# A two-stage image kernel: the convolution's loop written out as 24 chunks, and half of each output store moved behind the next matrix loads

## The chip, the cores and the metric

The kernel runs on one core of a Trainium2 chip. The metric is the device time of one execution in microseconds (us), median of several runs; less is better.

## What is computed

Two layers follow each other on an input of 4 images x 48 channels x 128 x 128 in float32. The first is a windowed transformer block (layer norm, attention in 8 x 8 windows, projection, layer norm, MLP with GELU, two residuals). The second, which the change touches, is an inverted bottleneck:

```python
h = jnp.einsum('oc,bchw->bohw', w1, x)                 # 48 -> 288 channels
h = jax.nn.relu(_bn(h, g1, b1, m1, v1))
h = jax.lax.conv_general_dilated(h, wd, (1, 1), ((1, 1), (1, 1)), feature_group_count=HID, ...)   # depthwise 3x3
h = jax.nn.relu(_bn(h, gd, bd, md, vd))
h = jnp.einsum('oc,bchw->bohw', w2, h)                 # 288 -> 48 channels
return x + _bn(h, g2, b2, m2, v2)
```

## The kernel before

Three stages run one after the other: `attention` (to about 770 us of the profile), `mlp` (to about 1100 us) and `conv` (to the end). `conv` shares its block of engine programs with `mlp`.

How `conv` is tiled. Each of the 4 images is cut into two halves of 64 columns, 8 halves in all (`HALVES`), and the 288 middle channels into 3 chunks of 96 (`CHUNKS`), so there are 24 chunks. A chunk has the number k = 3 x half + c; `number(b, hx, c)` works it out from the image b, the half hx in it and the chunk c. A half is 128 patches of 8 x 8 pixels, and one matmul of the depthwise step takes one channel with a matrix of its nine taps laid out for a patch (`mats`, three tiles of 32 channels, 896 KB each to load).

What TensorE does in chunk k (`chunk`, from L1147 on): depthwise units 1 to 5 of chunk k (`depthwise`, matmuls L1134, 160 of the chunk's 192), and then, in 8 steps (`NSTEP`), it expands the patches of chunk k + 1 (L1115), turns chunk k's result (transposes L1169) and projects it (L1160). Ahead of the last projection it does depthwise unit 0 of chunk k + 1. ScalarE and VectorE empty PSUM (L882, L883, L1216), and VectorE adds each projection to the output tile `y` (called `yc` in the profile): L1253 at c = 0, L1258 at c = 1, L1256 at c = 2. At c = 0 it overwrites what the half before left, so ahead of the first and of the fifth addition (n = 0 and n = 4, `PER_BLOCK` = 4) it waits on `y_stored[0]` and `y_stored[1]`, the stores of the first and the second 64 rows.

What GpSimd (POOL) does: it scales each loaded matrix tile in place (L932, `mats_scaled`), which TensorE waits for ahead of depthwise units 0, 2 and 4 of the next chunk, and it cuts the next half's image strips (`piece`) into patches `xp` (L906), at c = 1 and c = 2.

What SyncE (SP) does is the queue that the change reorders. SP's program is one list, and a wait in it holds up all that stands behind it. In chunk k, in this order:

1. three loads of `mats` for chunk k + 1 (L1073), each when TensorE has finished the depthwise units that read the tile (2, 4 and 6 of the 6 units; `unit_ready`);
2. at c = 0 and c = 1, eight strips each of the next half (`load_pieces`, L1065), two loads a strip; the second load of the first strip waits for the landing of the third matrix tile, the others for the strip before and for the cut that frees their slot;
3. at c = 2, the output of the half: for each of two blocks of rows a wait on `y_done` and two stores of 384 KB (L1082). The second block is complete at the end of the chunk, so its stores are followed at once by the matrix loads of the next half's first chunk.

All engines take the order of chunks from one helper, `schedule` (L801). It runs image 0, 1 and 2 (six chunks each, k = 0 to 17) as a hardware loop of three rounds (`eng.Fori`, L804) with the image's number in a register, so that the waits compare with values worked out in registers, and the last image (k = 18 to 23) as written-out code with constants. TensorE's loop body is six chunks long.

Of the kernel before, what the change touches and what calls it, by code (L numbers as in the profile page):

```python
# [29 lines left out]
B, C, H, W = 4, 48, 128, 128  # L30
# [18 lines left out]
PH, PW = 8, 8  # L49
# [7 lines left out]
CHUNKS = HID1 // CH  # L57
TCH = 32
LOADS = CH // TCH
HALVES = B * 2  # L60
# [6 lines left out]
def wait(eng, sem, n):  # L67

    if not isinstance(n, int) or n >= 1:
        eng.wait_ge(sem, n)  # L70
# [680 lines left out]
def conv(nc, d):  # L751


    with ExitStack() as ctx:
# [14 lines left out]
        PART = 8  # L769
# [10 lines left out]
        y = sb("yc", [P, PR * PH, PC // 2 * PW])  # L780
# [6 lines left out]
        mats_loaded = [sem(f"mats_loaded{s}") for s in range(LOADS)]  # L787
# [6 lines left out]
        y_ready, y_done, y_stored = sem("c_y_ready"), sem("c_y_done"), [sem(f"c_y_stored{k}") for k in range(2)]  # L794
# [4 lines left out]
        NSTEP = len(STEPS)  # L799

        def schedule(eng, first, chunk):  # L801

            first()
            with eng.Fori(0, HALVES // 2 - 1, 1) as b:  # L804
                for hx in range(2):
                    for c in range(CHUNKS):
                        chunk(b, hx, c, False)
            for hx in range(2):
                for c in range(CHUNKS):
                    chunk(HALVES // 2 - 1, hx, c, hx == 1 and c == CHUNKS - 1)  # L810

        LEAD = 3
        BLOCKS = PR // PART
        PER_BLOCK = NSTEP // BLOCKS
# [7 lines left out]

        def more(b, hx):

            return not (hx == 1 and isinstance(b, int))

        FIXED = 2 + 5 + 2 + SLOTS + 1 + 2 * SLOTS

# [4 lines left out]
        def pieces_at(c):  # L833
            return range(PR // 2 * c, PR // 2 * (c + 1))

        def nth_in_slot(j):
            return slot_of[:j].count(slot_of[j])

        def place_of(j):


            s = slot_of[j]
            before = [i for i in range(j) if slot_of[i] == s]
            return s, before[-1] + 1 if before else max(i for i in range(PR) if slot_of[i] == s) + 1 - PR
# [9 lines left out]
        def number(b, hx, c):  # L854
            return 2 * CHUNKS * b + CHUNKS * hx + c
# [9 lines left out]
        def ready_before_depthwise(k):  # L865
            return ready_before_expand(k) + EXPANDS
# [31 lines left out]
        block = ctx.enter_context(nc.Block(name="mlp_conv"))  # L898
# [36 lines left out]
        def piece_rows(j):  # L935

            lo, hi = max(PH * j - 1, 0), min(PH * j + PH + 1, H)
            return lo, hi, lo - (PH * j - 1)
# [106 lines left out]
        @block.sync  # L1045
        def _(sp):
            sp.wait_ge(fixed, FIXED)
            for s in range(2):
                sp.wait_ge(img_stored[s], 32 * (STRIPS // 2))

            def load_pieces(b, hx, h, c):

                k = CHUNKS * (h - 1) + c
                for j in pieces_at(c):
                    slot, nth = place_of(j)
                    wait(sp, cut, PR * h + nth)
                    lo, hi, off = piece_rows(j)
                    for r in range(2):
                        if r and j > pieces_at(c)[0]:
                            before = slot_of[j - 1]  # L1060
                            sp.wait_ge(piece_loaded[before], 32 * (PER_HALF[before] * (h - 1) + nth_in_slot(j - 1) + 1))
                        elif r:
                            sp.wait_ge(mats_loaded[-1], 16 * (k + 1))
                        x0 = HALF * hx + HALF // 2 * r
                        sp.dma_start(piece[slot][ONE * r:ONE * r + C, off:off + hi - lo, :],  # L1065
                                     d["img_images"][:, b, lo:hi, x0:x0 + SIDE]).then_inc(piece_loaded[slot], 16)

            def chunk(b, hx, c, last):
                k = number(b, hx, c)
                if not last:  # L1070
                    for s in range(LOADS):
                        sp.wait_ge(unit_ready, ready_before_depthwise(k) + READY[DEPTHS // LOADS * (s + 1)])
                        sp.dma_start(mats[s][0:MROWS, :, :], d["taps"][LOADS * ((c + 1) % CHUNKS) + s])\  # L1073
                            .then_inc(mats_loaded[s], 16)
                if c < 2 and more(b, hx):
                    load_pieces(b + hx, 1 - hx, 2 * b + hx + 1, c)
                if c == CHUNKS - 1:
                    for block in range(BLOCKS):
                        sp.wait_ge(y_done, NSTEP * k + PER_BLOCK * (block + 1) + 1)
                        rows = slice(PH * PART * block, PH * PART * (block + 1))  # L1080
                        for r in range(2):
                            sp.dma_start(d["out"][4 * b + 2 * hx + r].rearrange("c (y x) -> c y x", y=H)[:, rows, :],  # L1082
                                         y[64 * r:64 * r + C, rows, :]).then_inc(y_stored[block], 16)

            schedule(sp, lambda: None, chunk)
            for block in range(BLOCKS):
                sp.wait_ge(y_stored[block], 32 * HALVES + 32)

        @block.tensor
        def _(pe):  # L1090
# [57 lines left out]
            def chunk(b, hx, c, last):  # L1148
# [32 lines left out]
                for n in range(NSTEP + 1):  # L1181
# [7 lines left out]
                    if n < NSTEP:  # L1189
                        turn(n)  # L1190

            schedule(pe, first, chunk)

        @block.scalar
        def _(act):
# [23 lines left out]
            def first():  # L1219
                expanded(0, range(0, EXPANDS, 2))  # L1220
                for s in range(2):
                    act.wait_ge(img_stored[s], 32 * (STRIPS // 2))

            schedule(act, first, chunk)

        @block.vector
# [111 lines left out]
```

## Time and profile before

| | |
|---|---|
| median of 3 runs | 2005.19 us (2003.86 to 2009.8) |
| the profiled execution | 2007.32 us, its span 2005.3 us |
| TensorE busy | 1913.1 us, 95% of the span |
| VectorE, ScalarE, GpSimd busy | 72%, 68%, 32% |
| granted TensorE clock, mean | 0.991 |
| DMA | 198.73 MB, 99 GB/s over the span |

The profile is of one execution, its own time beside that of its span; what is worked out from rows is worked out for it. Engines: PE is TensorE's matmuls, PEld its weight loads, PEldq, DVEq, ACTq and SPq the engines' instruction queues, where branches, register operations and DMA issues show. `<-` in a tile column reads "out from in". The chain that ended last follows the execution back from its last instruction, at each step to what released it; "issue" is time in which the engine waited for nothing that the profile shows. In the DMA view, q1 holds the transfers issued by SP, q8 and q14 ("instruction") bring the engines' own code, in packets of 16 KB and 8 KB.

### The profile page before, as it was taken

The numbers are of one execution on the slowest core, as the hardware profiler recorded it, in microseconds if no ns is written. First come the engines' busy times: TensorE is split into PE (matmuls) and PEld (weight loads), VectorE is DVE, ScalarE is ACT, GpSimd is POOL, SyncE is SP. The second block draws the span as 40 slices with busy tenths as digits, with TensorE's granted clock in tenths as the row PEclk, the third lists the DMA queues.
The fourth block names the chain that finished last, engine by engine and source line by source line (L and its number), as shares of the span: only waits on it lengthen the run. The fifth ranks groups of instructions, "written<-read, shape, count | busy, mean of one in ns | idle before, by whom it ended". The sixth has DMA issues, their size and how long they took to land.

```text
span 2005.3 us, 76491 instructions
## 1 busy us (share of the span) xinstructions
PE 1913.1 (95%) x29704; PEld 1584.4 (79%) x29704; DVE 1441.9 (72%) x2586; ACT 1365.1 (68%) x2838; POOL 647.0 (32%) x869
## 2 busy tenths in 40 slices
PE   5999999999999996999999999999999999999998
PEld 4888888888888884555555898989989898999987
DVE  4999999999999995555556556656656565566554
ACT  2888888888888884666666566656666566666655
POOL 4333333333333336023000433424334243324240
PEclk9999999999999997999999999999999999999999
DMA  2222222222222224677554345435354454455431
GB/s 65 67 76 76 76 76 75 73 77 75 76 76 76 76 71 113 159 164 156 135 134 110 95 99 132 96 100 129 92 129 98 110 132 99 92 138 101 109 95 34
DMA packets 286441, 198.73 MB, mean 99 GB/s; under 512 B 225991, under 2 KB 275672, under 8 KB 276504
## 3 DMA queue, kind: packets, MB, share of 16 engines
q1 hardware_dynamic: 282114, 189.12, 37.7%
q0 software_dynamic: 2368, 6.25, 1.8%
q8 instruction: 154, 2.52, 0.6%
q10 hardware_dynamic: 1750, 0.39, 0.1%
q14 instruction: 55, 0.45, 0.1%
HBM read 128.36 MB, written 54.72 MB: 91 GB/s over the span
## 4 chain that ended last, share of the span: by engine, by line
PE 57%; ACT 2%; issue 1%; DVE 1%; DMA 0%; SPq 0%; ACTq 0%; DVEq 0%
PE psum L1115 14%; PE psum L1134 13%; PE psum L1160 9%; PE psum L676 6%; PE psum L661 6%; PE psum L1169 5%; PE psum L650 3%; ACT h2T L1216 1%; DVE h L883 1%; DMA room<-in_ident 0%; ACT room L742 0%; DVE room L883 0%; ACT room L746 0%; ACT h L882 0%; DVE room L708 0%
## 5 line engine op out<-in xcount | busy, mean ns | idle before, releaser
L932 POOL TENSOR_TENSOR mats<-mats,dscale 112x2048 f32<-112x2048 f32 x72 | 260.8, 3622 | 350.1 <-DMA mats<-in_taps 348.1
L1115 PE MATMUL psum<-ew,xp 64*100 64x96 f32 x6144 | 322.6, 253 | 15.5 <-DVE h L883 11.1
L1216 ACT ACTIVATE h2T<-psum 96x1024 f32<-96x1024 f32 x192 | 195.8, 1020 | 189.6 <-PE psum L1169 189.6
L883 DVE TENSOR_SCALAR h<-psum 100x384 f32<-100x384 f32 x384 | 212.0, 557 | 149.8 <-PE psum L1115 139.0
L1115 PEld LDWEIGHTS psum<-ew,xp 64*100 64x100 f32 x6144 | 295.3, 165 | 25.4 <-DVE h L883 14.1
L1134 PE MATMUL psum<-h,mats 101*64 101x128 f32 x4608 | 269.4, 276 | 6.8 <-issue 5.2
L1134 PEld LDWEIGHTS psum<-h,mats 101*64 101x64 f32 x4608 | 253.9, 138 | 15.5 <-issue 6.5
L882 ACT ACTIVATE room<-psum 64x512 f32<-64x512 f32 (+1 forms) x384 | 206.3, 537 | 85.1 <-PE psum L1134 78.7
L344 PE MATMUL psum<-kb,qa 128*64 128x256 f32 x2048 | 244.6, 381 | 0.6 <-DVE prob L443 0.6
L883 DVE TENSOR_SCALAR room<-psum 64x512 f32<-64x512 f32 (+1 forms) x288 | 174.1, 604 | 72.1 <-PE psum L1134 66.1
L882 ACT ACTIVATE h<-psum 100x384 f32<-100x384 f32 x384 | 186.7, 486 | 45.8 <-PE psum L1115 33.6
L1160 PE MATMUL psum<-h2T,pw 128*64 128x128 f32 x3072 | 196.7, 277 | 19.7 <-issue 10.2
L1160 PEld LDWEIGHTS psum<-h2T,pw 128*64 128x64 f32 x3072 | 167.9, 137 | 32.1 <-ACT h2T L1216 13.7
L344 PEld LDWEIGHTS psum<-kb,qa 128*64 128x64 f32 x2048 | 140.8, 138 | 56.2 <-issue 1.9
L526 POOL TENSOR_TENSOR xn<-cen,rstd 128x192 f32<-128x192 f32 x128 | 64.7, 506 | 339.9 <-ACT rstd L499 339.9
L436 DVE TENSOR_REDUCE top<-psum 128x16 f32<-128x1024 f32 x128 | 156.7, 1224 | 6.7 <-PE psum L344 4.3
L742 ACT ACTIVATE room<-psum,room 128x512 f32<-128x512 f32 x128 | 81.2, 686 | 112.8 <-PE psum L676 112.7
L443 DVE TENSOR_TENSOR prob<-psum,top 128x1024 f32<-128x1024 f32 x128 | 155.9, 1218 | 0.1
L471 ACT ACTIVATE probT<-psum 128x512 f32<-128x512 f32 x256 | 151.3, 601 | 0.0
L396 PE MATMUL psum<-vb,probT 128*64 128x26 f32 x4096 | 143.4, 219 | 1.6 <-issue 1.0
L396 PEld LDWEIGHTS psum<-vb,probT 128*64 128x64 f32 x4096 | 129.9, 138 | 18.7 <-issue 1.2
L906 POOL COPY xp<-piece 128x400 f32<-128x400 f32 x128 | 67.6, 528 | 226.0 <-DMA piece<-img_mid 223.6
(152 smaller groups left out, 3309.8 us busy)
## 6 DMA issues: line engine op xcount, KB each, us to landing
mats<-in_taps SPq DMA_DIRECT2D x69, 896.0 KB, 6.3
tok_mid<-mid SPq DMA_DIRECT2D x128, 224.0 KB, 1.9
room<-tok_mid SPq DMA_DIRECT2D x64, 448.0 KB, 3.8
piece<-img_mid SPq DMA_DIRECT2D x196, 63.8 KB, 2.3
img_mid<-room SPq DMA_DIRECT2D x128, 97.5 KB, 2.9
kb<-kk SPq DMA_DIRECT2D x512, 24.0 KB
out<-yc SPq DMA_DIRECT2D x32, 384.0 KB, 4.3
scratch<-in_x_tokens SPq DMA_DIRECT2D x126, 96.0 KB, 2.0
```

The costliest lines, as they stand in the source:

```text
L344: mm = nc.tensor.matmul(ps_s[NT * w:NT * w + NT, p // 2, 256 * (p % 2):256 * (p % 2) + 256], qa[s][:, NT * n:NT * n + NT], kb[s][:, n, :, ...
L396: mm = nc.tensor.matmul(ps_o[NT * w:NT * w + NT, at:at + 2 * VE], probT[:, p, h, NT * w:NT * w + NT], vb[1 - s][:, p, h, w, :], start=True ...
L436: nc.vector.tensor_reduce(top[s][:, :], sc, AX_X, ALU.max).then_inc(top_done, 1)
L443: nc.vector.tensor_tensor(prob[s][:, :, :], sc, bc(top[s][:, :], 2, NT), ALU.subtract)\
L471: nc.scalar.activation(probT[:, 2 * k:2 * k + 2, :, :].rearrange("q p h n -> q (p h n)"), ps_p[:, k, :], ACT.Copy)\
L882: return nc.scalar.activation(dst, src, ACT.Relu)
L883: return nc.vector.tensor_scalar(dst, src, 0.0, None, ALU.max)
L932: nc.gpsimd.tensor_tensor(m, m, bc(scale[0:MROWS, at:at + TCH], 2, POUT), ALU.mult).then_inc(mats_scaled, 1)
L1115: mm = nc.tensor.matmul(ring[(j + u) % 4][0:PIN, p:4 * CH:4], xp[hx][rows, 2 * j + p, :], w1[rows, c, :], start=True, stop=True)
L1134: mm = nc.tensor.matmul(bank[:, n % 4:4 * PATCHES:4], mats[ch // TCH][0:PIN + 1, ch % TCH, :], h1[0:PIN + 1, ch, :], start=True, stop=True)
L1160: mm = nc.tensor.matmul(ps_y[n % 2][64 * r:64 * r + 64, at:at + PCOLS], w2[:, c, :], h2T[n % 2][:, r, at:at + PCOLS], start=True, stop=True)
L1216: nc.scalar.activation(h2T[n % 2][0:CH, :, :], turned_at(n, last)[0:CH, :, 0:POUT * PART], ACT.Copy).then_inc(copied, 1)
```

## The change

`schedule` no longer has a loop: all engines' programs for the 24 chunks are written out one after the other, with constants in place of register values. `more`, which says whether there is a next half whose strips are to be loaded, is rewritten for that, with the same meaning.

SP's stores become a function `store(h, block)`. The first block of a half is still stored at the end of SP's part of chunk c = 2. The second block is stored in the next half's first chunk: behind its three matrix loads, after a wait until the third of them has landed (`mats_loaded[-1]`), and ahead of its strip loads. The last half stores both blocks at its end as before. Nothing else is changed: the same matmuls, transfers and semaphores.

```diff
--- before.py
+++ after.py
@@ -801,13 +801,8 @@
         def schedule(eng, first, chunk):
 
             first()
-            with eng.Fori(0, HALVES // 2 - 1, 1) as b:
-                for hx in range(2):
-                    for c in range(CHUNKS):
-                        chunk(b, hx, c, False)
-            for hx in range(2):
-                for c in range(CHUNKS):
-                    chunk(HALVES // 2 - 1, hx, c, hx == 1 and c == CHUNKS - 1)
+            for k in range(HALVES * CHUNKS):
+                chunk(k // (2 * CHUNKS), k // CHUNKS % 2, k % CHUNKS, k == HALVES * CHUNKS - 1)
 
         LEAD = 3
         BLOCKS = PR // PART
@@ -822,7 +817,7 @@
 
         def more(b, hx):
 
-            return not (hx == 1 and isinstance(b, int))
+            return 2 * b + hx + 1 < HALVES
 
         FIXED = 2 + 5 + 2 + SLOTS + 1 + 2 * SLOTS
 
@@ -1065,6 +1060,15 @@
                         sp.dma_start(piece[slot][ONE * r:ONE * r + C, off:off + hi - lo, :],
                                      d["img_images"][:, b, lo:hi, x0:x0 + SIDE]).then_inc(piece_loaded[slot], 16)
 
+            def store(h, block):
+
+                k = CHUNKS * h + CHUNKS - 1
+                sp.wait_ge(y_done, NSTEP * k + PER_BLOCK * (block + 1) + 1)
+                rows = slice(PH * PART * block, PH * PART * (block + 1))
+                for r in range(2):
+                    sp.dma_start(d["out"][2 * h + r].rearrange("c (y x) -> c y x", y=H)[:, rows, :],
+                                 y[64 * r:64 * r + C, rows, :]).then_inc(y_stored[block], 16)
+
             def chunk(b, hx, c, last):
                 k = number(b, hx, c)
                 if not last:
@@ -1072,15 +1076,15 @@
                         sp.wait_ge(unit_ready, ready_before_depthwise(k) + READY[DEPTHS // LOADS * (s + 1)])
                         sp.dma_start(mats[s][0:MROWS, :, :], d["taps"][LOADS * ((c + 1) % CHUNKS) + s])\
                             .then_inc(mats_loaded[s], 16)
+                if c == 0 and k:
+                    sp.wait_ge(mats_loaded[-1], 16 * (k + 1))
+                    store(k // CHUNKS - 1, 1)
                 if c < 2 and more(b, hx):
                     load_pieces(b + hx, 1 - hx, 2 * b + hx + 1, c)
                 if c == CHUNKS - 1:
-                    for block in range(BLOCKS):
-                        sp.wait_ge(y_done, NSTEP * k + PER_BLOCK * (block + 1) + 1)
-                        rows = slice(PH * PART * block, PH * PART * (block + 1))
-                        for r in range(2):
-                            sp.dma_start(d["out"][4 * b + 2 * hx + r].rearrange("c (y x) -> c y x", y=H)[:, rows, :],
-                                         y[64 * r:64 * r + C, rows, :]).then_inc(y_stored[block], 16)
+                    store(k // CHUNKS, 0)
+                    if last:
+                        store(k // CHUNKS, 1)
 
             schedule(sp, lambda: None, chunk)
             for block in range(BLOCKS):
```

## Rows read from the trace of the kernel before

**Rows 1.** The page, parts 1 (busy, share, instructions) and 3 (queue: packets, MB, share).

```profile
PE 1913.1 (95%) x29704; PEld 1584.4 (79%) x29704; DVE 1441.9 (72%) x2586; ACT 1365.1 (68%) x2838; POOL 647.0 (32%) x869
...
q8 instruction: 154, 2.52, 0.6%
```

**Rows 2.** The chain that ended last, 1080 to 2005 us: start us, us, what.

```profile
1198.15 8.91 PE psum L1134 x160
...
1234.02 8.97 PE psum L1134 x160
...
1250.47 2.27 issue
...
1272.43 8.91 PE psum L1134 x160
...
1308.20 8.91 PE psum L1134 x160
...
1343.97 2.76 issue
...
1384.70 8.91 PE psum L1134 x160
...
1472.69 1.70 issue
...
1565.62 2.41 issue
...
1693.73 3.07 issue
...
1824.14 9.06 PE psum L1134 x160
...
1860.06 9.06 PE psum L1134 x160
...
1895.99 9.13 PE psum L1134 x160
...
1912.92 2.91 issue
...
1936.73 9.06 PE psum L1134 x160
...
1972.65 7.26 PE psum L1134 x128
```

**Rows 3.** Lines L804 and L592 (mlp's loop): durations min/median/max ns, first and last start.

```profile
L804 PEldq COMPARE_BRANCH  x3: 83/3407/3752, 1342.8 to 1786.9; - x3
...
L592 PEldq COMPARE_BRANCH  x14: 76/208/221, 823.6 to 1082.0; - x14
```

**Rows 4.** DMA, 1244 to 1249.5 us: packets and MB; every queue that moved anything.

```profile
DMA packets 171, 1.24 MB, mean 225 GB/s; under 512 B 20, under 2 KB 20, under 8 KB 20
...
q1 hardware_dynamic: 170, 1.23, 99.2%
q14 instruction: 1, 0.01, 0.7%
```

**Rows 5.** Timeline of SP's DMA issues, 1232 to 1249 us: start, us, line.

```profile
1235.34 0.83 SPq L1082 DMA_DIRECT2D out<-yc  x2
1236.30 7.07 SPq L1073 DMA_DIRECT2D mats<-in_taps  x3
```

**Rows 6.** DMA by chunk (2; then 3; then 4, two rows): KB each, median us to landing.

```profile
out<-yc SPq DMA_DIRECT2D x2, 384.0 KB, 5.3
...
mats<-in_taps SPq DMA_DIRECT2D x3, 896.0 KB, 11.8
...
q8 instruction: 5, 0.08, 1.0%
...
mats<-in_taps SPq DMA_DIRECT2D x3, 896.0 KB, 6.2
```

**Rows 7.** Timelines of VectorE and GpSimd: fifth addition of chunk 3, scalings in chunk 4.

```profile
1265.45 0.69 DVE L1253 TENSOR_TENSOR yc<-psum,xp 128x512 f32<-128x512 f32 x1 [0.44 <-PE psum L1160]
...
1284.80 7.33 POOL L932 TENSOR_TENSOR mats<-mats,dscale 112x2048 f32<-112x2048 f32 x2 [1.28 <-DMA mats<-in_taps]
```

## The prediction

> **What bounds the kernel now.** I read the page first. TensorE is busy for 1913.1 of 2005.3 us [rows 1], so only what stops TensorE, or makes its own stream longer, moves the time. The change touches the convolution alone, so I went to the chain that ended last, from 1106 us on, and used it as a ruler. A chunk k (0 to 23; k % 3 == 0 opens a half) shows there as one piece of 160 depthwise matmuls, `PE psum L1134 x160`, and the distance from one such start to the next is what a chunk costs. A chunk in which nothing goes wrong takes 1308.20 - 1272.43 = 35.77 us inside the loop, and 1860.06 - 1824.14 = 35.92 us in the six chunks that are already written out behind it [rows 2]. From chunk 2 to chunk 23 there are 21 distances, 1972.65 - 1198.15 = 774.50 us, where 21 x 35.77 = 751.17. So 23.33 us of the convolution is excess, and the change can be worth no more than that.
>
> Where the excess sits is told by the pieces called "issue" in the same chain, time in which TensorE waited for nothing that the profile shows. There are six behind the first chunk [rows 2]: two at the loop's end (2.76 us at 1343.97, 2.41 us at 1565.62) and four in the first chunk of an odd half, k = 3, 9, 15 and 21 (2.27 us at 1250.47, 1.70 at 1472.69, 3.07 at 1693.73, 2.91 at 1912.92). The chunks around them lose more than the bare stall, as TensorE comes back slower than it left: k = 3 takes 1272.43 - 1234.02 = 38.41, 2.64 over; k = 21 takes 1936.73 - 1895.99 = 40.74, 4.82 over the 35.92 of a written-out chunk; the two chunks round the first loop end take 1384.70 - 1308.20 = 76.50, 4.96 over 2 x 35.77 [rows 2]. The second loop end I take in proportion to its stall, 4.96 x 2.41 / 2.76 = 4.3. The rest of the 23.33 is small: 0.10 at k = 2 (1234.02 - 1198.15 = 35.87), 0.75 for five written-out distances at 0.15, and 5.8 for k = 9 and 15 with crumbs (23.33 - 2.64 - 4.82 - 4.96 - 4.3 - 0.10 - 0.75 = 5.76).
>
> **Part 1, no loop.** The change removes two taken backward branches on each engine. TensorE's own takes 3752 ns, 3407 ns at the median of three and 83 ns where it falls through at the exit; the same branch of the stage before, whose body is four short steps, takes 208 ns [rows 3]. So it is not the branch that costs but what has to come after it, and the body of the convolution's loop is six chunks long. The trace has a DMA queue for it: q8 "instruction" brings blocks of 16 KB, 154 in all [rows 1], one per 7 us in this stage (five in the 35.8 us of chunk 4) [rows 6]. With the branches gone, 4.96 + 4.3 = 9.3 us go.
> The Trainium skill (Advanced Engine Details and Errata, Control Flow Timing) gives a compare-and-branch about 108 ns; by that the two branches would be worth 0.2 us. The 208 ns is near it and the 3752 ns is not, and the trace decides. The skill's Runtime: NRT & Kernel Launch, Instruction fetch mechanics, has the reason: a taken branch out of the blocks held starts a fetch that execution must wait for.
>
> What is added is the written-out stream's own price: 0.15 us a chunk (35.92 against 35.77; the x160 piece is 9.06 against 8.91 us) [rows 2]. It falls on the 18 chunks that leave the loop, +2.7 us. Bounds: 0, if short waits early in the code are cheaper than the late ones seen, to 2.7. I take 2.7, since every undisturbed written-out chunk shows it.
>
> **Part 2, the store behind the matrices.** Before, at the head of chunk k = 3h, SP sends the second part of the output (2 x 384 KB, issued 1235.34) and 0.1 us later the first of three loads of depthwise matrices (3 x 896 KB, issued 1236.30 to 1243.4) [rows 5]. In chunk 4, without a store ahead, such a load lands in 6.2 us at the median, in chunk 3 in 11.8 [rows 6]. Nearly 3.5 MB lie in the queue, and the 16 DMA engines are full (q1 has 99.2%) from 1244 to 1249.5. In these 5.5 us there is a block for another queue (q14), but no q8 row at all [rows 4]. That alone would say little at one block per 7 us, but 0.97 us behind the window TensorE stalls for 2.27 us [rows 2]. I read this as: a block of TensorE's code comes late because of the pile in the DMA engines, and TensorE runs out of instructions. All four stalls stand in opening chunks, which alone have a store ahead of their loads; the chunks away from these and from the loop's ends have none.
>
> After the change the opening chunk's loads meet what they meet in every other chunk: they are issued at the same moments (they wait for TensorE's own progress, at 1236.3, 1239.5, 1243.1) and land about 6.2 us after the last, at 1249.3 instead of 1254.8. So I expect these stalls to go, k = 3: 2.64, k = 21: 4.82, k = 9 and 15 with the crumbs: 5.8 and 0.10 at k = 2; 13.4 in all.
>
> What takes its place: SP now waits for the third matrix load before it stores. Behind it on SP's queue stand the two stores and the pieces of the next half's image. The pieces lose nothing: the second load of the first piece waited for that very landing already (1254.8), and now goes some 5 us earlier, behind 768 KB of store, which is 3.5 us at the 225 GB/s of the busy window [rows 4]. The store lands about 5.3 us after its issue, as the first part does with nothing beside it [rows 6], so near 1249.3 + 1.2 + 5.3 = 1255.8; VectorE writes that part of y again from its fifth addition of the chunk, at 1265.45 [rows 7]. Slack 9.6 us; if it were gone, the excess would go straight to the time. Matrices are scaled by 1284.80 + 7.33 = 1292.1 in chunk 4 [rows 7] and wanted some 3 us ahead of the piece at 1308.20 [rows 2], 13 us later, so a load that slips by 1 us costs nothing. The store's own burst can still hold up a code block. The nearest row is the first part's store, alone at 1222.8: its chunk, k = 2, is 0.10 over [rows 2]. The other end is that TensorE stands for as long as 768 KB take less the time by which a block is early, which I bound by half the 3.5 us. Seven boundaries: 0.7 to 12 us; I take 0.7, as that row is of the same transfer on the same queue. Below nothing it can't go, because the 21 x 35.77 already has no stall in it.
>
> **Sum.** Gone 9.3 + 13.4 = 22.7; added 2.7 + 0.7 = 3.4; net 19.3 us. The profiled execution took 2007.3 us (span 2005.3), 2.1 above the median of the runs, 2005.19; it would become 1988.0. Against the median: 2005.2 - 19.3 = 1985.9 us, 0.96% faster.
>
> **The rivals.**
> *The store's burst stalls TensorE instead.* The backlog is cut in two, and the second half still hits some blocks: 0.7 becomes up to 12 us, 1985.9 to 2005.2 - 22.7 + 2.7 + 12 = 1997.2. For it: the burst is now pressed between matrices and pieces, and TensorE is there in its expand part, where small matmuls eat a block fastest. Against it: k = 2.
> *The order does nothing.* The late block has another cause (its place in the code, say), the stalls of the opening chunks stay and only the loop ends go: 2005.2 - 9.3 + 2.7 = 1998.6; if the even halves, freed of the loop, then get a stall of the mean size too, (2.64 + 4.82 + 5.8) / 4 = 3.3 at three boundaries, 2008.5. For it: chunk 18 opens a half too, with the same store and loads, already written out, and the chain has no "issue" in it. Against it: of the five opening chunks away from a loop end (3, 9, 15, 18, 21) it is the only one.
> The Trainium skill has a rule that would give this result: DMA: Bandwidth & Descriptors, Queues, rings and completion order, says that an engine goes round its queue rows after each packet. Then a code block would never wait for the whole pile and the order of transfers on SP's queue could not matter. The missing q8 row speaks against it here, the clean chunk 18 for it.
> *Slower: every opening chunk stalls as the written-out one does.* Chunk 21 is the only disturbed chunk without a loop around it, and it is the worst, 4.82 us. If straight code has its blocks in the same place of each half and the store's burst (which now starts near 15.5 us into the chunk, where the four stalls lay at 16 to 17) falls on the same block, all seven boundaries pay it: 7 x 4.82 = 33.7 in place of the 13.4, so 2005.2 - 9.3 + 2.7 + 33.7 - 13.4 = 2018.9. It decides from 22.7 - 2.7 = 20 us, that is from 2.9 us a boundary.
>
> **How the numbers follow.** The stalls go: 0.62, at 1985.9 with a span of 1982 (no straight-code price: 1985.9 - 2.7 and 0.7 less of burst) to 1990. The burst stalls: 0.18, 1990 to 1998. The order does nothing: 0.14, 1998.6 to 2008.5. Slower: 0.05, 2019. Lower than 1982: 0.01. 1982 to 1998 holds 0.80; I go to 1998.6, the near end of the third. Within 0.3% is about what a measurement of this kernel can tell from no change, 1999.2 to 2011.2. Faster: 0.62 + 0.18 + 0.01 and a fifth of the 0.14 = 0.84; same 0.11; slower 0.05.
>
> **What would show it.** In the chain of the changed kernel: no "issue" near a loop end, since no branch is taken; depthwise starts 35.92 us apart throughout (35.77 would say that straight code is free); at opening chunks the matrix load lands in 6 to 7 us, not 11, with a q8 row in the first 5.5 us after them, and no "issue" 15 to 20 us into the chunk. If those are there at 18 to 20 us, the burst rival holds; at 16 to 17 us with matrices landed early, the cause was never the pile. I am wrong altogether if VectorE's L1253 waits for a DMA of `out`, or if TensorE's L1134 waits for POOL.

## The result, and the profile after

The changed kernel takes 1985.47 us at the median of 4 runs (1984.52 to 1987.11), against 2004.53 for the kernel before (4 runs, 2003.74 to 2009.8): 19.1 us less, a ratio of 0.990 with a 95% interval of 0.9882 to 0.9919. The profiled execution took 1985.67 us, its span is 1983.9 us. The forecast was 1985.9.

The chain that ended last, in the changed kernel (start us, us, what; L1138 is the depthwise matmul, L1134 before), against [rows 2]:

```profile
1105.48 2.21 issue
...
1197.82 9.07 PE psum L1138 x160
1233.74 9.13 PE psum L1138 x160
1269.73 9.07 PE psum L1138 x160
1305.66 9.07 PE psum L1138 x160
1341.59 9.13 PE psum L1138 x160
...
1952.71 7.26 PE psum L1138 x128
```

From 1108 us on there is no "issue" of a microsecond or more left. The 2.21 us at 1105.48 is the entry into the stage, which both kernels have. A chunk takes 35.93 us (1305.66 - 1269.73) or, if it opens a half, 35.99 (1269.73 - 1233.74), and nothing else occurs: from chunk 2 to chunk 23 it is 1952.71 - 1197.82 = 754.89 us, where it was 774.50. Of the 21.4 us between the two spans 19.6 lie there. Another 1.5 us is in the last chunk (31.2 us from its start to the end of the span, 32.7 before), where the chain of before goes through a late emptying by VectorE and that of after doesn't. The third and fourth experiments, with the store moved as well, have 32.5 and 32.7 us there and the second, with the store in its old place, 31.2, so that part doesn't come from the change.

SP's issues in the opening chunk 3 (start, us, line), against [rows 5]:

```profile
1235.76 7.46 SPq L1077 DMA_DIRECT2D mats<-in_taps  x3
1248.68 0.79 SPq L1069 DMA_DIRECT2D out<-yc  x2
1249.52 12.76 SPq L1060 DMA_DIRECT2D piece<-img_mid  x9
```

The DMA view of the same chunk, 1233.57 to 1269.56 us (KB each, median us to landing), against [rows 6]:

```profile
q8 instruction: 5, 0.08, 1.0%
...
mats<-in_taps SPq DMA_DIRECT2D x3, 896.0 KB, 5.8
...
out<-yc SPq DMA_DIRECT2D x2, 384.0 KB, 4.5
```

The matrix loads land in 5.8 us, not 11.8, and the third is in at 1248.6, where it was 1254.8 before. Of the two parts of the store the second is in at 1254.4. VectorE writes that block of `y` again at its fifth addition:

```profile
1262.76 0.69 DVE L1257 TENSOR_TENSOR yc<-psum,xp 128x512 f32<-128x512 f32 x1 [0.44 <-PE psum L1164]
```

It waited 0.44 us for TensorE and not for the store: 8.4 us of slack, 9.6 forecast.

### The profile page after: what moved, and what is told of

Same layout as the page of the kernel before. It is cut to its first block, busy times and chain, and to the rows that moved or that the text cites. A ratio compares the mean times of both kernels' runs of the same rounds, so it can differ in the third digit from the quotient of the medians.

```text
span 1983.9 us, 74128 instructions
## 1 busy us (share of the span) xinstructions
PE 1907.0 (96%) x29704; PEld 1580.2 (80%) x29704; DVE 1442.4 (73%) x2586; ACT 1365.9 (69%) x2838; POOL 648.1 (33%) x869
## 3 DMA queue, kind: packets, MB, share of 16 engines
q1 hardware_dynamic: 282114, 189.12, 37.3%
## 4 chain that ended last, share of the span: by engine, by line
PE 57%; ACT 2%; issue 0%; DVE 0%; DMA 0%; SPq 0%; ACTq 0%; DVEq 0%
PE psum L1119 14%; PE psum L1138 13%; PE psum L1164 9%; PE psum L676 7%; PE psum L661 6%; PE psum L1173 5%; PE psum L650 3%; ACT h2T L1220 1%; ACT h L877 1%; DMA room<-in_ident 0%; ACT room L742 0%; ACT room L746 0%; DVE room L878 0%; DVE room L708 0%; ACT L742 0%
## 5 line engine op out<-in xcount | busy, mean ns | idle before, releaser
L1138 PE MATMUL psum<-h,mats 101*64 101x128 f32 x4608 | 269.2, 274 | 1.6 <-issue 0.9
L1138 PEld LDWEIGHTS psum<-h,mats 101*64 101x64 f32 x4608 | 252.1, 137 | 11.7 <-issue 2.0
L877 ACT ACTIVATE h<-psum 100x384 f32<-100x384 f32 x384 | 186.7, 486 | 46.5 <-PE psum L1119 32.7
```

What stands on the lines that cost most here:

```text
L877: return nc.scalar.activation(dst, src, ACT.Relu)
L1138: mm = nc.tensor.matmul(bank[:, n % 4:4 * PATCHES:4], mats[ch // TCH][0:PIN + 1, ch % TCH, :], h1[0:PIN + 1, ch, :], start=True, stop=True)
```

## The experiments

All are judged by two measures: the median of the runs, and the distance from the depthwise of chunk 2 to that of chunk 23 in the profiled execution ("the 21 distances": 774.50 us before, 754.89 after). What a chunk lost is its distance less that of a clean one. Chips differ: on those of the experiments the kernel before had medians of 2008.8 (first group), 2008.8 (second) and 2005.9 (third), over a spread of 13 to 22 us. The changed kernel, run again in the second group, had 1986.6.

| kernel | median us (range) | 21 distances | opening chunks 3, 6, 9, 12, 15, 18, 21 |
|---|---|---|---|
| before | 2004.5 to 2008.8 | 774.50 | 38.4, 37.8*, 37.9, 37.3*, 39.2, 36.1, 40.7 |
| changed | 1985.5; again 1986.6 | 754.89; 755.3 | all 35.99 (again: one of 36.35) |
| e1 loop, store moved | 1998.2 (1991.5 to 2003.2) | 767.42 | 36.8, 37.3*, 37.3, 37.8*, 37.2, 37.5, 36.9 |
| e2 written out, old store | 2000.8 (1995.8 to 2006.3) | 771.52 | 37.4, 38.4, 40.9, 39.7, 38.9, 37.4, 36.0 |
| e3 no wait | 1988.6 (1987.9 to 1989.4) | 756.54 | 36.0 but 36.8 at 15 and 18 |
| e4 pile in the middle | 1990.3 (1987.5 to 1990.6) | 759.28 | 36.0 but 36.6 at 12 |
| e5 one matrix wait | 1986.4 (1985.4 to 1989.3) | 755.3 | all 35.99 |
| e6 loop ends mid-half | 2002.7 (1998.2 to 2006.6) | 772.02 | 36.5, 39.9*, 35.8, 40.1*, 36.3, 35.8, 36.0 |
| e7 old store, whole block | 2015.2 (2005.9 to 2020.3) | 771.4 | 38.8, 40.0, 40.1, 36.0, 39.9, 37.6, 36.0 |
| e8 waits swapped | 1985.8 (1984.6 to 1986.2) | 754.5 | all 35.94 |
| e9 old store, half block | 2012.7 (2005.7 to 2022.7) | 769.66 | 41.3, 40.9, 38.8, 36.5, 37.2, 36.1, 36.0 |
| e10 changed, half block | 1990.8 (1990.2 to 1992.5) | 754.88 | all 35.99 |
| e11 store first, no pile | 1990.4 (1987.5 to 1993.9) | 760.96 | 36.0 but 36.7 at 9 |

A star marks a chunk with a loop end at one of its borders.

**One part at a time.** e1 keeps the loop and moves the second store of the even halves only, behind the loads of chunks 3, 9, 15 and 21:

```diff
+                if c == 0 and hx == 1:
+                    sp.wait_ge(mats_loaded[-1], 16 * (k + 1))
+                    for r in range(2):
+                        sp.dma_start(d["out"][4 * b + r]...[:, PH * PART:, :], y[64 * r:64 * r + C, PH * PART:, :])...
...
-                    for block in range(BLOCKS):
+                    for block in range(1 + hx):
```

> Part 2 alone: the loop stays, and the second store goes behind the three matrix loads at the opening chunks of the odd halves (k = 3, 9, 15, 21), which are those that stalled. Theory (a block of TensorE's code comes late because of the pile of store and loads): the four stalls go, the two at the loop's end stay, 2004.5 - 2.6 - 4.8 - 5.7 = 1991.4 us. Rival (order does nothing, the gain of the change is all the loop's and something else in the written-out code): 2004.5 us, with stalls at the same four places. Rival (the burst behind the loads stalls TensorE): stalls of 1 to 3 us at 18 to 20 us into those chunks.

Measured 1998.2 us, a ratio to before of 0.9949 (0.9931 to 0.9966), 10.5 us less where 13 was expected. The four stalls went from 2.6, 2.1, 3.5 and 4.8 us to 1.0, 1.6, 1.4 and 0.9. Chunk 3 of e1 in the chain (1233 to 1271 us):

```profile
1233.53 8.98 PE psum L1143 x160
...
1249.99 0.60 issue
```

and SP's store in the same chunk:

```profile
1250.52 0.87 SPq L1086 DMA_DIRECT2D out<-yc  x2
```

The chunk lost 1.0 us at 16.5 us into it, and the stall begins 0.5 us before the store is issued. So it isn't the store's burst; the matrix loads, 7.8 us to landing at the median, were alone ahead of it. In chunks 9 and 15, 0.6 to 0.7 us were lost at 17 us, about 1 us behind the issue of the store, and 0.9 us at 23.4 us; chunk 21 lost 1.1 us in one step at 23.6 us. Of these, the losses at 23 us and more stand right behind the store's landing (23.0 to 23.3 us), and there the burst rival holds, in small; those at 17 us are ahead of the same instruction as the one in chunk 3 and may be the loads'. The loop ends kept their 4.2 and 4.7 us. Chunks 6, 12 and 18 have their store in the old place here.

e2 writes the chunks out and leaves the store where it was:

```diff
-                if c == 0 and k:
-                    sp.wait_ge(mats_loaded[-1], 16 * (k + 1))
-                    store(k // CHUNKS - 1, 1)
...
-                    store(k // CHUNKS, 0)
-                    if last:
-                        store(k // CHUNKS, 1)
+                    for block in range(BLOCKS):
+                        store(k // CHUNKS, block)
```

> Part 1 alone: 24 chunks written out, both stores of a half where they were, ahead of the next matrix loads. Theory: the two loop-end stalls go and the price of written-out code is paid, with stalls left in opening chunks: between 1998.6 us (four of them as before) and 2008.5 us (all seven at the mean size); at every one of the seven the third matrix load lands in 11 us. Rival (the stalls belonged to the looped code, the order of the transfers is idle): 1986 us as the full change. Rival (every boundary as chunk 21): 2019 us.

Measured 2000.8 us, ratio 0.996 (0.9946 to 0.9975), within the expected band. The loop ends are gone, but six of seven boundaries now stall, the even ones too (2.4, 3.7 and 1.4 us at 6, 12 and 18), 16.6 us in all. TensorE's code is here the same, instruction for instruction, as in the changed kernel, so that the stretch behind the depthwise of chunk 9 can be laid side by side. The chain of e2:

```profile
1452.35 9.13 PE psum L1134 x160
...
1467.61 3.00 issue
```

DMA of e2 in the 8.6 us ahead of that stall, 1459 to 1467.6 us:

```profile
q1 hardware_dynamic: 268, 1.95, 99.3%
```

DMA of the changed kernel in the same stretch of the same chunk, 1456.1 to 1464.7 us:

```profile
q1 hardware_dynamic: 254, 1.77, 70.6%
q8 instruction: 1, 0.02, 0.9%
```

Same code, same place: with the pile no block of code comes in 8.6 us and TensorE stands; without it the block comes and TensorE goes on. The two kernels differ in nothing but the place of 768 KB in SP's list and the wait ahead of it. The block that e2 lacked is transferred next (DMA of e2, 1467.6 to 1469.3 us), and TensorE goes on at 1470.61, 1.4 us behind its landing:

```profile
q8 instruction: 1, 0.02, 5.3%
```

The same is seen at every stall. Counted over all of TensorE's instructions in the trace, there are 34 places in the chunks of the written-out kernels (e2, e3, e4, e7, e9, e11) where 0.3 us or more is lost in one step. All 34 stand at an instruction whose number leaves 121 to 123 when divided by 256, and at each TensorE goes on 1.2 to 1.7 us after a packet of q8 has landed. So these are stalls for code, and a block is 256 instructions. In chunk 9 both kernels pass the boundary ahead 9.3 us into the chunk; the packet for the next block starts 10.6 us into it in the changed kernel and 15.7 us in e2.

A stall can cost more than its length. In e2's chunk 9 the stall of 3.0 us costs 4.9, for behind it TensorE's granted clock is 0.50, the lower of its two levels, for 3 us (DMA share and GB/s are the last two numbers, the clock stands ahead of them):

```profile
1470.60:1473.60 3.00, 2.99 (x31) 2.82 (x33) 1.11 (x2) 0.98 (x2) 3.00 (x1) 0.50 0.14 34
```

In chunk 12 of e2 a stall of 3.2 us left the clock at 1.00, and the chunk lost 3.7. What decides between the two isn't shown.

**Pile or order.** e3 is the changed kernel without SP's wait, so that the store is issued right behind the third load:

```diff
                 if c == 0 and k:
-                    sp.wait_ge(mats_loaded[-1], 16 * (k + 1))
                     store(k // CHUNKS - 1, 1)
```

> The changed kernel without SP's wait for the landing of the third matrix tile: the two stores of the second block are issued right behind the third load. As much data is piled up, but the matrices are ahead. Theory 1 (what counts is how much lies in the DMA engines when TensorE wants its next block, 13 to 16 us into the chunk): some of the stalls come back, 1988 to 2000 us. Theory 2 (what counts is only that the store is not ahead of the loads): 1985.5 us, no stall, and the third load lands in 6 to 7 us.

1988.6 us; two of seven chunks lost 0.8 us. The loads landed in 6.1 us, the store in 6.8. Closer to theory 2: putting the matrices first does most of it. The wait brings at most the last 2 us (1986.6 in the second group, on another chip, with 1987.4 as its slowest run; e3's fastest is 1987.9); in the 21 distances it is 1.2 to 1.7 us, and another 1.3 us is in the last chunk, as above.

e11 has the old order but no pile: store first, each transfer waiting for the one ahead to land.

```diff
                     for s in range(LOADS):
+                        if c == 0 and k:
+                            sp.wait_ge(*((mats_loaded[s - 1], 16 * (k + 1)) if s else (y_stored[1], 32 * (k // CHUNKS) + 32)))
                         sp.wait_ge(unit_ready, ready_before_depthwise(k) + READY[DEPTHS // LOADS * (s + 1)])
```

> Written out, second store ahead of the loads as before, but in opening chunks SP waits for the store to land before the first matrix load and for each load before the next, so that the order is the old one and nothing piles up. Theory (the pile, not the order): no stall in opening chunks, 1986.6 us, the last tile lands some 21 us into the chunk and is scaled by 25, ahead of its use at 33. Rival (a store ahead of the loads stalls TensorE by itself): 8 to 17 us of stalls as in the second experiment, 1995 to 2003 us.

SP's issues in chunk 3:

```profile
1233.50 0.78 SPq L1069 DMA_DIRECT2D out<-yc  x2
1239.03 12.55 SPq L1079 DMA_DIRECT2D mats<-in_taps  x3
1251.62 0.42 SPq L1060 DMA_DIRECT2D piece<-img_mid  x1
```

The opening chunks are clean but one (0.7 us, against 16.6 us over six of them in e2): a store ahead of the loads does little harm if nothing is piled on it, and that settles pile against order. The time is still 1990.4, between theory and rival. The strips now start late (1251.62) and run into the next chunk's matrix loads (the first issued 5 us into chunk 4, not 2), and the middle chunks 4, 10, 13, 16 and 19 lose 0.3 to 1.4 us each. There the pile had only moved by one chunk. Chunk 17 lost 0.6 us with its loads at their usual time.

e4 makes a pile where there was none, ahead of the middle chunks' loads:

```diff
+                if c == 1 and k > 1:
+                    for r in range(2):
+                        sp.dma_start(d["spare"][2 * (k // CHUNKS) + r],
+                                     d["taps"][0][0:C].rearrange("q c o -> q (c o)")).then_inc(spared, 16)
```

> The changed kernel with a new pile at a place that never stalled: ahead of the matrix loads of each middle chunk (k = 4, 7, ..., 22) SP issues two copies of 384 KB from the tap table to a spare tensor, nothing waits for them before the end. It adds this work and takes nothing away. Theory (pile delays code blocks): loads there land in 10 to 12 us, and some or all of the seven chunks get an issue stall of 1.7 to 3.1 us, 2.1 to 4.8 us each all told, so 1990 to 2019 us. Rival (stalls hang on the place in the code or on the first chunk of a half): none, 1985.5 us.

1990.3 us, 3.7 over the changed kernel. The stall in chunk 4, and the chunk's DMA view (1268.57 to 1306.34 us):

```profile
1284.11 1.48 issue
```

```profile
mats<-in_taps SPq DMA_DIRECT2D x3, 896.0 KB, 9.6
```

Three of the piles cost something: 1.8 us at chunk 4, 0.6 at 10, 1.3 at 16; the three at 7, 13 and 19 nothing, and at 22 the copy was issued so early that it met no load. A pile makes a stall in a chunk that never had one, so it isn't the place in the program alone. Small losses come without a pile too: 0.7 us at chunk 12 here, 0.4 us at chunk 12 in the repeat of the changed kernel, 0.4 us at chunk 7 in e5. The size was expected larger: the copies land in 4.6 us here and the loads in 9.6, not 11.8, a smaller pile than the real one.

**Where the blocks fall.** e7 and e9 are e2 with 64 and 32 idle matmuls ahead of TensorE's first expand; e10 is the changed kernel with 32.

```diff
                 pe.wait_ge(border_set, 2)
+                for n in range(32):
+                    nc.tensor.matmul(ring[0][0:PIN, 0:4 * CH:4], xp[0][0:ONE, 0, :], w1[0:ONE, 0, :], start=True, stop=True)
```

> Written out, both stores in the old place, and 64 idle matmuls (128 instructions, 3.6 us, results overwritten) ahead of TensorE's first expand, which moves all that follows by half a 16 KB block of code. Theory (a stall needs the pile and a block that falls due in it; the pile is there at all seven boundaries): the sizes at the seven boundaries are other ones than in the kernel without the shift (1.4, 2.4, 4.9, 3.7, 2.9, 1.4, 0), still 5 to 25 us in all. Rival (the place in the code alone decides): either all gone or all of one size. Rival (place is idle, luck of the moment alone): sum near 17 us.

The 64 matmuls were a slip: each leaves two matmuls and two weight loads in the trace, 256 instructions, so that they make a whole block and shift nothing. The run is then a repeat of e2 with 11.5 us of idle work in front, and is of use as that: the sum of the seven stalls is 16.5 us in the profile against 16.6, but the sizes are others (2.8, 4.0, 4.1, 0, 4.0, 1.6, 0 against 1.4, 2.4, 4.9, 3.7, 2.9, 1.4, 0). The same code in the same place under the same pile stalls by different amounts. (By the medians e7 is 14.4 us above e2, 2.9 more than the idle work, over a spread of 14 us.)

> Written out, stores in the old place, with 32 idle matmuls, which is really half a 16 KB block (the 64 of the run before were a whole block, as each is carried out in two passes, and its blocks fell as without them). Costs some 4 us by itself at its place. Theory (a stall needs a pile and a block that falls due in it): other sizes at the seven boundaries, and another sum than the 16.6 us that both placings without a shift showed; anything from 5 to 30 us. Rival (the moment alone decides): 16.6 us again within 3 us.

> The changed kernel with the same half block of shift ahead of TensorE's first expand. If the clean opening chunks (35.99 us) owe something to where the blocks fall, the burst of the store, now at 16 to 21 us of the chunk, costs about 1 us in each of the seven, as with the loop in the first experiment (0.9 to 1.5): 7 to 10 us over the 791 us of chunks 1 to 22. If the moved store is harmless wherever blocks fall: 791 us, and the time is 1986.6 plus the 4 us that the idle matmuls take.

e9: 5.3, 4.9, 2.8, 0.5, 1.2, 0.1 and 0 us, 14.7 in a profile that was of the fastest of its ten runs, a median of 2012.7. e10: not one chunk disturbed, and 1990.8 within 2.3 us. Its chain:

```profile
1202.36 9.07 PE psum L1138 x160
1238.29 9.13 PE psum L1138 x160
1274.28 9.07 PE psum L1138 x160
...
1957.24 7.26 PE psum L1138 x128
```

The 4.2 us over 1986.6 are the idle matmuls, which hold TensorE for 5.9 us; from the first expand to the end of the span it is 875.2 us in e10 and 875.2 in the changed kernel. So the moved store is harmless in both placings of the written-out code.

The shift does show in where e9 stalls. Numbering a chunk's weight loads from the first of its 160 depthwise matmuls, TensorE stands ahead of load 375 in chunk 3 and of load 293 in chunk 9 of e2, and ahead of 311 and 228 in e9: 64 and 65 loads earlier, half a block, as a load and its matmul are two instructions. In e7, with its whole block, the stalls from chunk 6 on are ahead of loads 269, 293, 341 and 365, as in e2. So the place in the code does decide where in a chunk a stall can stand, and the pile whether one comes and how long it is. The sums say less: e9's profiled execution was 7.0 us faster than its median, and less the 5.9 us of idle work that median is 6.0 us above e2's, so 14.7 is likely too low for e9. With a spread of 17 us and the two on record in different groups, a larger sum isn't shown.

**The loop ends.** e6 brings the loop back round chunks 1 to 6, with all stores in the new order, so that its ends lie one chunk behind the boundary:

```diff
+            chunk(0, 0, 0, False)
+            with eng.Fori(0, HALVES // 2 - 1, 1) as b:
+                for k in range(1, 2 * CHUNKS + 1):
+                    chunk(b + k // (2 * CHUNKS) if k == 2 * CHUNKS else b, *place(k), False)
```

> The changed order of SP's list at all boundaries, but with the hardware loop back: chunk 0 written out, then three rounds of chunks 1 to 6, so that the two taken branches lie between chunks 6 and 7 and 12 and 13, far from any store. Theory (a taken branch costs 4.1 to 5 us by itself, and the loop's chunks 35.78): 1985.5 + 2 x 4.3 - 17 x 0.15 + some us of burst in the opening chunks, as they showed with the loop in the first experiment (4 x 1.2) = 1991 to 1996 us. Rival (a good part of the loop-end cost came from the store beside it): 2 us or less a branch, 1987 to 1990 us.

2002.7 us, far over both. TensorE's branch and the chain round the first loop end:

```profile
L806 PEldq COMPARE_BRANCH  x3: 83/3462/3839, 1378.1 to 1825.3; - x3
...
1379.23 2.47 issue
1382.54 2.04 issue
```

The branch takes what it took [rows 3], but a second stall stands 0.8 us behind the first: the block behind the target isn't there either. Its q8 packet lands at 1383.3, and TensorE goes on at 1384.6; the DMA engines are nearly idle in that stretch (a share of 0.04 from 1381.7 to 1384.6), so no pile is in play. The two loop ends cost 8.7 and 9.7 us (chunks 6 and 7: 39.85 + 40.47 - 35.84 - 35.78), twice the 4.96 of [rows 2], without a store beside them. Part of that is again the clock: it is granted at 0.50 from 1384.6 to 1388.5 us here, and at 0.52 from 1346.7 to 1350.0 us behind the first loop end of the kernel before. So the loop-end cost isn't borrowed from the store, and it depends on where the loop is cut. The opening chunks with the moved store lose 0.7 us at 3 and 0.5 at 15 and next to nothing at 9, 18 and 21.

**The price of written-out code.** e5 and e8 look for the 0.15 us a chunk.

```diff
-                if d % (DEPTHS // LOADS) == 0:
-                    pe.wait_ge(mats_scaled, LOADS * k + d // (DEPTHS // LOADS) + 1)
+                if d == 0:
+                    pe.wait_ge(mats_scaled, LOADS * (k + 1))
```

> The changed kernel, but TensorE waits for the three scaled matrix tiles with one wait ahead of depthwise unit 0, in place of one each ahead of units 0, 2 and 4. The tiles have been ready for some 13 us by then. If the price of written-out code (0.15 us a chunk) lies in these extra waits in front of units that already carry two, the chunk takes 35.77 us and the kernel 1985.5 - 24 x 0.15 = 1982 us. Rival (the price lies elsewhere, in the fetching of more code or in constants): 35.93 us a chunk, 1985.5 us.

35.92 to 35.93 us a chunk (chunk 7 alone 36.35), 1986.4 us: it isn't the number of waits on the matrices.

```diff
-                pe.wait_ge(unit_act, act_before_depthwise(k, d))
                 pe.wait_ge(unit_dve, dve_before_depthwise(k, d))
+                pe.wait_ge(unit_act, act_before_depthwise(k, d))
```

> The changed kernel with the two waits ahead of a depthwise unit in the other order (VectorE's first, ScalarE's last). In the loop the last wait before the unit's first weight load was on VectorE's semaphore, in written-out code it is on ScalarE's, with VectorE's in an instruction of its own of 51 ns ahead of it; units 3 and 5 start 0.07 us later each. If that order is the price of written-out code: 35.77 us a chunk, 1986.6 - 24 x 0.15 = 1983 us. Rival (an instruction of its own costs it, whichever semaphore it is): 35.93 us, 1986.6 us.

35.92 us again (opening chunks 35.94, 0.05 less), 1985.8 us. The weight loads of unit 3 now start as early as in the loop, 0.06 us earlier than without the swap, but the time is lost again by the end of the first expands. The price follows neither; in the loop the first wait of a pair rides on a register operation of 32 ns, in written-out code it is an instruction of 51 ns, and which of these is the cause stays open.

## Why the prediction was right

- **The ruler and the bound.** The excess of 23.33 us over clean chunks was the most there was to win; 19.6 of it, net of the written-out price, was won. One reading by it was too general: that TensorE "comes back slower than it left". In chunk 3 the granted clock stays at 1.00 and all but 0.1 us of the 2.64 is lost in one step at the stall. In chunk 21 it is true: 3.3 us at the stall, and the other 1.5 at a clock of 0.50 from 1917 to 1920 us.
- **The loop ends, 9.3 us** (9.1 by the distances of all four chunks). Gone, since no branch is taken. The reading that the cost comes from fetching code behind the branch is borne out by e6, where both stalls at a loop's end are over 1.3 to 1.5 us after a q8 packet has landed. The Trainium skill (Runtime: NRT & Kernel Launch, Instruction fetch mechanics) says that a branch out of the two blocks at hand breaks the sequential prefetch; the 3.4 to 3.8 us of both loops agree, and the 0.1 us of its Control Flow Timing list (Advanced Engine Details and Errata) doesn't agree with them.
- **The written-out price, 0.15 us a chunk.** 35.93 as read off the last image before.
- **The opening chunks, 13.4 us.** Gone, by the mechanism named: e2 against the changed kernel shows the missing block on identical code, e4 makes a stall by a pile, e11 takes all but 0.7 us of them away without touching the order. The forecast of this step rested on one window without a q8 row and four places, too little to be sure by; that it held was in part luck.
- **The burst, 0.7 us forecast for seven boundaries.** 0.4 at most (35.99 against 35.93), and even that isn't the burst's: chunk 21 of e2, e7 and e9, with no stall and the store in its old place, takes 35.99 as well. In e1, 0.9 to 1.6 us are lost at chunks 9, 15 and 21 with the store under way or just landed. Why there stays open. It isn't the loop's code alone, as chunk 21 of e1 stands in written-out code; its store lands 23 us into the chunk, that of the changed kernel 21. The upper bound of the forecast was of use.
- **The slacks.** Store to the fifth addition 8.4 us (9.6 forecast), strips and scaled matrices in time.

The split of the sum was less good than the sum. The forecast treats the parts as independent: 6.6 us net for the loop, 12.7 for the store. On the way over e1 the profiles give 7.1 for the four stores that it moves and 12.5 for the loop with the other three, over e2 3.0 for the loop and 16.6 for the store. The step that was incomplete is "the loop ends are 9.3 us and the rest stays": where a loop ends, the even half's own stall stays small, and e2 shows these (7.4 us at 6, 12 and 18) once the loop is gone. Only with both parts do the two sums meet. The same goes for chunk 18, which I had taken as the strongest evidence against the pile: it lost 1.5 us in e1, with its store in the old place, and 1.4 in e2. Its clean pass in the profile of before was one draw; a pile is a risk, not a fixed cost. The rival that "the order does nothing" is out by e2; and the slower one needed every boundary at 4.8 us, where two at most reached it.

The Trainium skill's rule that a DMA engine goes round its queue rows after each packet (DMA: Bandwidth & Descriptors, Queues, rings and completion order) would let a code block pass the pile. 8.6 us without one at 99.3% load, where the same code without the pile had one, don't agree with it. Whether the rule doesn't cover the queue that brings code, or the block was asked for later than the trace lets one see, isn't shown.

## What to carry to other kernels

TensorE code as long as this is fetched while it runs, in blocks of 256 instructions, and its packets share the DMA engines with the data. Here 3.5 MB issued within 8 us starved it. The sign is an "issue" gap with DMA near 100% and no instruction packet ahead of it, which ends 1.2 to 1.7 us after the next such packet has landed. Put what isn't needed soon (an output store) behind what is, with a wait for the landing; in the written-out kernel that is worth 16.6 us. Write out a loop whose body is thousands of instructions if its ends cost more than the written-out code: here some 8800 instructions a round, 9.1 us against 2.7. Compare chunk by chunk against a clean chunk of the same trace: the excess is the bound of what can be won.

## What the runs showed beyond that

The moved store takes the scatter out as well. Kernels with the pile spread over 10 to 22 us from run to run in the experiments (before 2000.3 to 2013.4 in 19 runs of the first group, e9 2005.7 to 2022.7 in 10), those with the new order, no loop and no added piles over 1.5 to 3.9 us (changed 1984.9 to 1987.4 in 4 runs, e10 1990.2 to 1992.5 in 10). e11, with the old order and no pile, spread over 6.4 us in 8. A loop end's cost depends on where the loop is cut: 4.1 to 5.0 us ahead of chunk 6 or 12, 8.7 and 9.7 us one chunk later.
